# High and low halves interleaved element by element in a four-layer graph network kernel

## The reference

```
layer 0 (attention): Wh = h W;  e = leaky_relu(Wh a1 + (Wh a2)^T);  p = softmax(where(adj > 0.5, e, -9e15), axis=1)
                     x += elu(p Wh)
layer 1:             Ah = adj + I;  d = rsqrt(sum(Ah));  x += relu((d Ah d) h K1 + bias)
layer 2:             x += relu(adj h K2) * mask(rows of h that are not all zero)
layer 3:             agg = (adj h) / max(sum(adj), 1e-6);  x += relu([h, agg] W3^T)
```

## Time and profile before

| | |
|---|---|
| median of 3 runs | 2623.15 us (2622.8 to 2623.39) |
| the profiled execution, its own time | 2621.74 us |
| its span, first to last instruction | 2619.9 us |
| mean granted TensorE clock | 0.992 |
| TensorE / weight loads / VectorE / ScalarE / GpSimd busy | 97% / 84% / 70% / 54% / 45% |
| matmuls | 13704 |

### The profile page before, as it was taken

The page is one execution under the profiler, slowest core; times in us unless marked ns, Lnnn a source line. Parts: engine busy times, 40 slices in busy tenths (PEclk is TensorE's granted clock), DMA queues, the critical chain, the costliest instruction groups (busy, mean ns, idle before and its releaser), DMA issues.

```text
span 2619.9 us, 40393 instructions
## 1 busy us (share of the span) xinstructions
PE 2547.1 (97%) x13704; PEld 2205.5 (84%) x13704; DVE 1823.2 (70%) x4251; ACT 1408.7 (54%) x2571; POOL 1185.2 (45%) x1607
## 2 busy tenths in 40 slices
PE   2799999999999999999999999999999999999998
PEld 2688888888888888888888888888888888888886
DVE  6776676676676677677677777777776766766753
ACT  3555555555555555555555555555555555555542
POOL 2544444444444444444444444444444444444431
PEclk8899999999999999999999999999999999999999
DMA  4101111111011011011111111111111111111000
GB/s 140 41 29 49 33 41 49 33 41 49 30 44 49 29 45 49 29 45 46 33 45 41 37 45 41 37 45 35 42 46 33 41 49 33 41 49 33 29 17 25
DMA packets 72844, 109.30 MB, mean 42 GB/s; under 512 B 4288, under 2 KB 37056, under 8 KB 72640
## 3 DMA queue, kind: packets, MB, share of 16 engines
q1 hardware_dynamic: 72640, 106.71, 12.6%
HBM read 73.14 MB, written 33.55 MB: 41 GB/s over the span
## 4 chain that ended last, share of the span: by engine, by line
PE 96%; DVE 1%; issue 1%; ACT 1%; POOL 1%; DMA 0%; SPq 0%; POOLq 0%; ACTq 0%; DVEq 0%
PE O L277 46%; PE T L277 34%; PE X L277 13%; PE X L310 2%; PE X L298 1%; POOL h_lo L747 0%; ACT h L405 0%; DMA act_out<-w_all 0%; POOL xs L712 0%; DVE p_lo L589 0%; DVE scores L522 0%; DVE w_lo L512 0%; DVE t_lo L595 0%; ACT act_out L436 0%; DVE xs L630 0%
## 5 line engine op out<-in xcount | busy, mean ns | idle before, releaser
L747 POOL TENSOR_TENSOR h_lo<-h,h_hi 128x512 fp32r<-128x512 f32 x384 | 503.4, 1333 | 673.1 <-ACT h_hi L411 673.1
L595 DVE TENSOR_TENSOR t_lo<-T,t_hi 128x512 fp32r<-128x512 f32 x512 | 352.5, 690 | 399.1 <-ACT t_hi L417 399.1
L405 ACT ACTIVATE h<-xs,ln_bias,ln_scale 128x512 f32<-128x512 f32 x512 | 396.0, 811 | 391.9 <-POOL ln_bias L741 391.9
L277 PE MATMUL O<-w_hi,t_hi 128*128 128x512 f32 x1536 | 603.2, 393 | 0.0
L277 PE MATMUL O<-w_hi,t_lo 128*128 128x512 f32 x1536 | 598.2, 389 | 0.0
L277 PE MATMUL O<-w_lo,t_hi 128*128 128x512 f32 x1536 | 598.1, 389 | 0.0
L417 ACT CAST t_hi<-T 128x512 fp32r<-128x512 f32 x512 | 298.3, 584 | 257.1 <-PE T L277 257.1
L712 POOL TENSOR_TENSOR xs<-xs,act_out 128x512 f32<-128x512 f32 x128 | 163.7, 1297 | 531.7 <-ACT act_out L439 496.9
L277 PEld LDWEIGHTS O<-w_hi,t_lo 128*128 128x128 f32 x1536 | 288.3, 188 | 60.2
L277 PEld LDWEIGHTS O<-w_hi,t_hi 128*128 128x128 f32 x1536 | 288.5, 188 | 55.9 <-DVE t_lo L595 0.5
L277 PEld LDWEIGHTS O<-w_lo,t_hi 128*128 128x128 f32 x1536 | 288.6, 188 | 55.7
(11 more groups left out here) (92 smaller groups left out, 4991.4 us busy)
## 6 DMA issues: line engine op xcount, KB each, us to landing
xs<-x SPq DMA_DIRECT2D x64, 512.0 KB, 3.6
out<-xs SPq DMA_DIRECT2D x64, 512.0 KB, 2.8
a_raw<-adj_t SPq DMA_DIRECT2D x64, 256.0 KB, 2.7
a_rows<-adj SPq DMA_DIRECT2D x64, 256.0 KB, 2.7
xs<-w_all SPq DMA_DIRECT2D x6, 512.0 KB, 7.3
act_out<-w_all SPq DMA_DIRECT2D x2, 512.0 KB, 6.7
z<-w_all SPq DMA_DIRECT2D x2, 512.0 KB, 6.4
v_rows<-a_vecs SPq DMA_DIRECT2D x1, 512.0 KB, 5.4
```

Source lines behind the costliest of these rows:

```text
L277: last = nc.tensor.matmul(psum, s, m, start=(start and n == 0 and i == 0), stop=(stop and n == len(pairs) - 1 and i == 2))
L405: nc.scalar.activation(h[:, k.odd, m], xs[:, k.xb, m], ACT.Relu, bias=ln_bias[:, k.quad, m:m + 1], scale=ln_scale[:, k.quad, m:m + 1], acc ...
L595: nc.vector.tensor_tensor(t_lo[:, k.odd, c], T[:, c], t_hi[:, k.odd, c].bitcast(F32), ALU.subtract).then_inc(t_lo_ready, 1)
L747: nc.gpsimd.tensor_tensor(h_lo[:, k.odd, m], h[:, k.odd, m], h_hi[:, k.odd, m].bitcast(F32), ALU.subtract).then_inc(h_lo_ready, 1)
```

## The change

`h`, `t`, `ht` and `a` are no longer two tensors. Each becomes one tensor with an innermost dimension of 2, so that in memory a high element is followed by its low element; `_hi` and `_lo` are views with a step of two elements. `w` and `p` stay as they are. In layer 3, where `t` is the moving operand, the same memory is used in another way: the first half of a buffer holds the high values contiguously and the second half the low ones (`u_hi`, `u_lo`). The unused tensors change their sizes (96 to 112 floats behind the weights, a new one of 112 behind `a`, 48 to 64 before `p`). No instruction is added, removed or moved.

```diff
-        distance = sb("distance", [P, 96])
+        w_distance = sb("w_distance", [P, 112])
...
-        a_hi = sb("a_hi", [P, A_BUFS, NT, N], F32R)
-        a_lo = sb("a_lo", [P, A_BUFS, NT, N], F32R)
+        a_split = sb("a_split", [P, A_BUFS, NT, N, 2], F32R)
+        a_hi, a_lo = a_split[:, :, :, :, 0], a_split[:, :, :, :, 1]
+        a_distance = sb("a_distance", [P, 112])
...
-        h_hi = sb("h_hi", [P, 2, NT, F], F32R)
-        h_lo = sb("h_lo", [P, 2, NT, F], F32R)
-        t_hi = sb("t_hi", [P, 2, FT, N], F32R)
-        t_lo = sb("t_lo", [P, 2, FT, N], F32R)
-        ht_hi = sb("ht_hi", [P, FT, N], F32R)
-        ht_lo = sb("ht_lo", [P, FT, N], F32R)
+        h_split = sb("h_split", [P, 2, NT, F, 2], F32R)
+        t_split = sb("t_split", [P, 2, FT, N, 2], F32R)
+        ht_split = sb("ht_split", [P, FT, N, 2], F32R)
+        h_hi, h_lo = h_split[:, :, :, :, 0], h_split[:, :, :, :, 1]
+        t_hi, t_lo = t_split[:, :, :, :, 0], t_split[:, :, :, :, 1]
+        ht_hi, ht_lo = ht_split[:, :, :, 0], ht_split[:, :, :, 1]
+        u_split = t_split[:].rearrange("p b f n s -> p b (f n s)").rearrange("p b (s m n) -> p b s m n", s=2, m=NT)
+        u_hi, u_lo = u_split[:, :, 0], u_split[:, :, 1]
...
-        p_distance = sb("p_distance", [P, 48])
+        p_distance = sb("p_distance", [P, 64])
...
-                        u = slice(HALF * m, HALF * m + HALF)
-                        parts.append((a_hi[:, k.ab, m, c], a_lo[:, k.ab, m, c], flat(t_hi[:, k.odd, u]), flat(t_lo[:, k.odd, u])))
+                        parts.append((a_hi[:, k.ab, m, c], a_lo[:, k.ab, m, c], u_hi[:, k.odd, m], u_lo[:, k.odd, m]))
...
-                nc.scalar.copy(t_hi[:, k.odd, c], T[:, c]).then_inc(t_hi_ready, 1)
+                if k.layer == 3:
+                    nc.scalar.copy(u_hi[:, k.odd, b], flat(T[:, c])).then_inc(t_hi_ready, 1)
+                else:
+                    nc.scalar.copy(t_hi[:, k.odd, c], T[:, c]).then_inc(t_hi_ready, 1)
...
-                nc.vector.tensor_tensor(t_lo[:, k.odd, c], T[:, c], t_hi[:, k.odd, c].bitcast(F32),
-                                        ALU.subtract).then_inc(t_lo_ready, 1)
+                if k.layer == 3:
+                    nc.vector.tensor_tensor(u_lo[:, k.odd, b], flat(T[:, c]), u_hi[:, k.odd, b].bitcast(F32),
+                                            ALU.subtract).then_inc(t_lo_ready, 1)
+                else:
+                    nc.vector.tensor_tensor(t_lo[:, k.odd, c], T[:, c], t_hi[:, k.odd, c].bitcast(F32),
+                                            ALU.subtract).then_inc(t_lo_ready, 1)
```

## The result

The changed kernel takes 3024.52 us (median of 4 runs, 3022.51 to 3024.79) against 2623.09 us. The ratio is 1.1535, with a 95% interval of 1.152 to 1.1549. I had forecast 2518 us, and 2480 to 2700 as the range. Both are wrong, and so is the sign.

What follows compares the result with a forecast made beforehand. TensorE was taken to bound the kernel by its start-to-start distances. Gains of 1.32 + 0.21 + 0.16 = 1.69 us per graph, times 61.9, gave 105 us off 2621.7, so 2518 us with the median's offset; range 2480 to 2700.

Steps and rivals of the forecast that it cites:

- the excess of 11.1 and 13.4 ns: Time per matmul of 256 and 512 columns beyond its columns at 2.4 GHz; 2.60 us per graph with gather_last.
- The writers at nothing: Engines writing t, h, ht and a at every second element: from 0 to twice the duration, taken as 0.
- the possible doubling: Rival: strided writes take twice as long, VectorE becomes the bound, some 2600 us; chance 0.08.
- Ordering and DMAs at nothing: Ordering, DMAs, waits and instruction counts stay the same, loads still landing in contiguous a_raw: no change in time.
- the excess lies on the feeding side: TensorE's excess comes from a limit on the side feeding the array, since it is gone at 1.2 GHz.
- the 2.4 ns that went into the sum: Excess over the columns that the transposes keep, assumed to remain per matmul: 215.7 ns for 512 columns, 109.1 for 256.
- Stationary h beside moving a (48): Gathers over a, both operands interleaved: 8.7 ns gained or lost per matmul, 0.42 us per graph either way; taken as nothing.
- The forecast's own range: Times if the forecast mechanism holds: 2462 us (no excess at all) to 2560; 2480 to 2560 holds nearly all.
- with the halves interleaved the load takes the same rate, the two never slide: Weight load and moving stream both take 16 bytes in 4 cycles, so whether they meet depends on their first bytes.
- half a period apart everywhere: Changed pads put w, a, p at 0 and h, t, ht at 256 in a period of 512 bytes.
- 11 ns to gain per `w` matmul: Interleaved stationary t and ht beside contiguous w: 120 matmuls per graph gain 11.0 ns each, 1.32 us.
- rival of doubled meetings: Interleaved loads touch 64 pieces of 16 bytes instead of 32, excess beyond 2.4 ns doubles: +131 us, 2754 us; chance 0.19.

Runs made afterwards that it cites:

- the matrix: No layer computed: 49 sets of 24 fp32r matmuls with varied steps and first bytes; contiguous 226.7 ns, stationary step 2 233.3 ns at 256 bytes apart.
- new_pads_only: Kernel before, every tensor contiguous, with the changed kernel's three pads (112, 112, 64 floats): 2629.28 us, ratio 1.0031.
- w_off_64: Changed kernel with a contiguous again and the pad behind the weights at 128 instead of 112 floats: 2659.01 us, ratio 1.0141.
- t_off_16: Kernel before, contiguous, pads of 112 floats behind w, 48 before t, 64 before p, then t and ht 16 bytes further: 2649.67 us, ratio 1.0107.
- before_w_off_64: Kernel before with only the pad behind the weights changed, 112 instead of 96 floats: 2650.85 us, ratio 1.0112.

## Why the prediction was wrong

**What held.** TensorE as the only bound, the counts, the start-to-start distances as the measure, and the excess of 11.1 and 13.4 ns. The writers at nothing, against the possible doubling. Ordering and DMAs at nothing. That the excess lies on the feeding side: at 1.2 GHz it is gone, and with a repeated moving element all but 2.5 ns of it is gone at 2.4 GHz too (215.8 ns). One reading was a little off: the 0.108 us of the earlier trace rows is 1.6 ns beyond 128 columns at two cycles, and the 2.4 ns that went into the sum would need 0.109; that is under 8 us of the forecast.

**The step that failed most: "Stationary h beside moving a (48)".** I bounded it by 8.7 ns gained and 8.7 ns lost and took nothing; it is 113.8 ns lost, 5.46 of the 6.41 us per graph. The bounds came only from the meetings of two readers. I had written that the interleaved moving operand "takes 16 bytes in 2 cycles" without asking whether that rate can be delivered. The rows had a hint: contiguous fp32 at 2.4 GHz is already slower than its columns, and not at 1.2 GHz, so the stream was at its limit of supply, and a step of two spreads its elements over twice as many 16-byte pieces. The upper bound had to be twice the columns: 48 x (213.3 - 117.8 ns) = 4.6 us per graph, 284 us. The forecast's own range would then have ended beyond 2800 us.

The Trainium skill's SBUF — State Buffer (cachelines) says that two hits per 16-byte line keep full bandwidth. I used it as comfort. For a moving fp32 operand the runs here differ, and the measurement decides: two elements of each 16 bytes took 453.3 ns instead of 226.7. For bf16 at step 2, which uses four elements of 16 bytes, 225.8 ns is near full rate.

**The mechanism: "with the halves interleaved the load takes the same rate, the two never slide".** It is refuted. With a stationary step of 2 none of the distances tried reached 216 ns; the best was 230.0, worse than the best contiguous one. The runs fit an excess that is mostly the moving stream's own: no set of 512 contiguous fp32 columns was below 226.7 ns whatever the stationary operand, this is the 1.77 ns per 16-byte piece at which the strided sets run, and the excess vanishes only with the moving operand's reads. The weight load moves the distance by 0 to 12 ns on top, by its step and the two first bytes. But no set ran without a weight load beside it, so that none of the 13.4 ns is the load's is not shown. So there were no 11 ns to gain per `w` matmul, and 6.6 ns and more were lost. The period, which I took as 512 bytes with "half a period apart everywhere", is 256 in the matrix: the changed pads set the interleaved t and ht at distance 0, one of their worst (233.4), where contiguous ones are at their best (226.7). My rival of doubled meetings forecast the direction for `w`, 226.7 up to 240, but its reason, a count of pieces, is refuted as well, so its nearness is luck.

**How the 401 us divide, by the runs.** Putting back `a` gives 340 us; interleaving it alone costs 344. The rest, 63 us, is interleaving h, t and ht together with the pads: of that the pads by themselves are 8 us on the contiguous layout (new_pads_only), and 25 us is the choice of the distance for `w` (w_off_64).

**What stays open.** Why one and the same pair of first bytes has two steady rates, 113.3 and 117.8 ns for 256 columns and 226.7 and 233.3 for 512. The matmuls ahead seem to decide it, since moving t and ht alone changed the gathers, and in t_off_16 the rate goes by the piece ahead, but no run isolates that. So the table of distances holds for its own order of sets, and pads read from it are a guess for another stream. What repeats every 256 bytes no run shows.

## What to carry to other kernels

Keep a moving fp32 operand in runs of at least 16 bytes; where one tensor is moving in one product and stationary in another, lay it out for the moving role, since beside 512 columns the stationary one loses a few ns by a step of two and the moving one loses half its rate. When a stream already runs below the array's rate and comes up to it at the low clock, it is limited by supply: bound every layout that spreads its bytes by the 16-byte pieces that it touches. If interleaving is needed for other reasons, interleave in runs of 4 fp32 values on the moving side (233.3 ns for 512 columns against 453.3 element by element).

## What the runs showed of the hardware

- Moving operand, 512 columns at 2.4 GHz: fp32 contiguous 226.7 ns, step 2 453.3, step 3 453.4, step 4 460; runs of 2 453.4, of 4 and 8 233.3, of 16 240.2, of 64 228.0; bf16 steps 1 to 4: 215.9, 225.8, 340.0, 451.7; one repeated fp32 element 215.8. By the Trainium skill (TensorE: Matmul & The Clock Gate, Back-to-back issue gap) the distance at the full clock is columns/2.4 + 2.5 ns. The repeated element and bf16 at step 1 agree with it, contiguous fp32 does not.
- The Trainium skill (TensorE: Matmul & The Clock Gate, Step-by-step) says that weight loads take no bandwidth from the running matmul. Here a change of the stationary step or first byte alone moved the distance between 226.7 and 238.7 ns.
- Stationary fp32 step 4 costs little beside 512 columns (235.0 ns) but bounds narrow ones: 256 columns took 233.3 ns instead of 120.0, and 128 columns 233.9 instead of 111.7.
- A pad of 64 bytes in SBUF changed a whole kernel by 1.1% (before_w_off_64).
